# Two of the four loads of x issued by ScalarE in place of SyncE, in a graph-attention layer

## The reference

```python
x (8192, 64) f32;  adj (8192, 8192) int32, about 4 edges in a row;  W (64, 64);  a (128, 1)
h  = maximum(layernorm(x, axis=-1, eps=1e-5), 0)
Wh = h @ W
a1, a2 = a[:64, 0], a[64:, 0]
e  = leaky_relu((Wh @ a1)[:, None] + (Wh @ a2)[None, :], 0.2)
scores = where(adj > 0, e, -9e15)
attention = softmax(scores, axis=1)
out = x + elu(attention @ Wh)
```

## Time and profile before

| | us |
|---|---|
| median of three executions | 654.71 |
| the profiled execution, its own time | 654.69 |
| its span, first to last instruction | 652.8 |
| TensorE busy | 618.5 (95%) |
| VectorE busy | 614.8 (94%) |
| ScalarE busy | 623.9 (96%) |
| GpSimd busy | 81.6 (13%) |
| time in packets of the loads of `adj`, share of 16 DMA engines over the span | 98.6% |

### The profile page before, as it was taken

How to read it: one execution, slowest core, us unless ns; L and a number is a source line. 1 busy time by engine, 2 the same in 40 slices (tenths; PEclk the granted TensorE clock), 3 DMA queues, 4 the chain that set the end, 5 groups by cost and what they waited for, 6 DMA issues and landing times.

```text
span 652.8 us, 23363 instructions
## 1 busy us (share of the span) xinstructions
PE 618.5 (95%) x10422; PEld 607.1 (93%) x10422; DVE 614.8 (94%) x651; ACT 623.9 (96%) x357; POOL 81.6 (13%) x149
## 2 busy tenths in 40 slices
PE   4878999999999999999999999999999999989997
PEld 4748999999999999999899999999999999989997
DVE  5899999999999999889999999999999999999997
ACT  5799999899999999999999999999999999999992
POOL 7200200110110110100010110101010110011000
PEclk9987999999999999999999999999999999999999
DMA  9999999999999999999999999999999999999994
GB/s 173 109 108 109 110 108 108 110 109 109 109 108 108 107 107 108 108 108 108 107 108 108 108 108 107 108 107 108 108 108 107 108 107 108 108 108 107 107 97 132
DMA packets 27678, 71.81 MB, mean 110 GB/s; under 512 B 3200, under 2 KB 11136, under 8 KB 27648
## 3 DMA queue, kind: packets, MB, share of 16 engines
q0 software_dynamic: 18576, 67.12, 98.6%
q1 hardware_dynamic: 8608, 4.19, 2.4%
q10 hardware_dynamic: 464, 0.07, 0.1%
HBM read 270.60 MB, written 2.10 MB: 418 GB/s over the span
## 4 chain that ended last, share of the span: by engine, by line
ACT 53%; DMA 17%; PE 12%; issue 9%; DVE 7%; ACTq 1%; POOL 1%; DVEq 0%
ACT work L520 37%; DMA store<-in_adj 16%; ACT work L528 14%; DVE store L721 4%; PE psum L1083 3%; PE psum L1081 3%; PE psum L1061 2%; PE psum L1050 1%; PE psum L1028 1%; ACT last_steps L533 1%; DVE store L739 1%; DVE work L745 1%; DMA x_sb<-in_x 1%; PE psum L1018 1%; ACT V L512 1%
## 5 line engine op out<-in xcount | busy, mean ns | idle before, releaser
L520 ACT ACTIVATE work<-trow,Wh 128x4096 int8<-128x4096 f32 x128 | 494.6, 3867 | 0.0
L1081 PE MATMUL psum<-V,work 128*128 128x130 f16 x4096 | 479.3, 220 | 1.2 <-DVE work L745 1.2
L1083 PE MATMUL psum<-V,work 128*128 128x130 f16 x4096 | 479.2, 220 | 0.0
L1081 PEld LDWEIGHTS psum<-V,work 128*128 128x128 fp8e4 x4096 | 401.9, 98 | 1.5 <-issue 1.5
L1083 PEld LDWEIGHTS psum<-V,work 128*128 128x128 fp8e4 x4096 | 401.8, 98 | 0.0
L721 DVE TENSOR_SCALAR store<-store 128x4096 uint8<-128x4096 int8 x127 | 290.2, 2286 | 4.4 <-DMA store<-in_adj 4.4
L739 DVE SCALAR_TENSOR_TENSOR store<-work,store 128x1024 int32<-128x1024 int32 x128 | 156.5, 1222 | 12.7 <-ACT work L520 10.0
L528 ACT COPY work<-psum 128x1024 int32<-128x1024 int32 x128 | 147.5, 1155 | 7.6 <-PE psum L1061 7.4
L1061 PE MATMUL psum<-identb,store 128*128 128x128 bf16 x2048 | 135.7, 220 | 16.3 <-DVE store L739 13.4
L1061 PEld LDWEIGHTS psum<-identb,store 128*128 128x128 bf16 x2048 | 119.6, 98 | 20.1 <-DVE store L739 10.7
L443 POOL DMA_DIRECT2D store<-in_adj x127 | 71.2, 561 | 510.9 <-DVE store L721 503.3
(11 more groups left out here) (90 smaller groups left out, 146.6 us busy)
## 6 DMA issues: line engine op xcount, KB each, us to landing
store<-in_adj POOLq DMA_DIRECT2D x127, 512.0 KB, 27.6
x_sb<-in_x SPq DMA_DIRECT2D x4, 512.0 KB, 6.2
out_y<-x_sb SPq DMA_DIRECT2D x1, 1792.0 KB, 8.0
store<-in_adj POOLq DMA_DIRECT2D x2, 256.0 KB, 35.3
out_y<-x_sb SPq DMA_DIRECT2D x1, 128.0 KB, 6.0
out_y<-x_sb SPq DMA_DIRECT2D x4, 32.0 KB, 1.6
store<-in_L_gnn_W ACTq DMA_DIRECT2D x4, 16.0 KB, 5.3
a_sb<-in_L_gnn_a ACTq DMA_DIRECT2D x1, 0.5 KB, 4.2
```

The costliest lines, as they stand in the source:

```text
L520: nc.scalar.activation(sign[:, k % 2].bitcast(I8), trow[:, h * UW:(h + 1) * UW], ACT.Sign, bias=(Wh[:, B, 0:1] if isinstance(B, int) else ...
L1081: nc.tensor.matmul(sums_of[:, 0], up8[:, j // 2, j % 2], V[:, jb, 0:FP], start=begins and j == 0, stop=False, skip_group_check=True)
L1083: last = nc.tensor.matmul(sums_of[:, 1], down8[:, j // 2, j % 2], V[:, jb, VP:VP + FP], start=False, stop=stops and j == HB - 1, skip_grou ...
```

## The change

ScalarE issues the loads of the second and fourth quarter of `x`, ahead of its five small loads; SyncE issues those of the first and third. Tiles, semaphores, sizes and everything else stay. Lines behind the change move down by five in the changed kernel.

```diff
             def _(sp):
                 xs = x.rearrange("(g p b) f -> p g b f", p=P, b=2)
                 with nc.allow_non_contiguous_dma(reason="pairs of rows of x, 512 bytes each"):
-                    for r in range(NR):
+                    for r in range(0, NR, 2):
                         sp.dma_start(x_sb[:, out_of(r), :].rearrange("p (g b) f -> p g b f", b=2),
                                      xs[:, r * PR:(r + 1) * PR]).then_inc(s_x[r], 16)
...
             @block.scalar
             def _(act):
                 act.sem_inc(s_codeT, TWO)
+                xs = x.rearrange("(g p b) f -> p g b f", p=P, b=2)
+                with nc.allow_non_contiguous_dma(reason="pairs of rows of x, 512 bytes each"):
+                    for r in range(1, NR, 2):
+                        act.dma_start(x_sb[:, out_of(r), :].rearrange("p (g b) f -> p g b f", b=2),
+                                      xs[:, r * PR:(r + 1) * PR]).then_inc(s_x[r], 16)
                 with nc.allow_non_contiguous_dma(reason="128 numbers"):
                     act.dma_start(a_sb[:, :], a.rearrange("(c f) o -> f (c o)", c=2)).then_inc(s_a, 16)
```

## The result

The changed kernel takes 657.54 us (median of 5, 656.95 to 657.81) against 654.71 (654.53 to 655.17): ratio 1.0042, 95% interval 1.0031 to 1.0053. The profiled execution has a span of 655.7 us, 2.9 more than before, and ScalarE is the place to look first.

What follows compares the result with a forecast made beforehand. The prediction took the stream of `adj` loads, set by tile 0's landing, as the bound. First `adj` load +0.91 us, less 0.1 saved at start-up, gave +0.8: 654.7 + 0.8 = 655.5 us, range 654.4 to 657.2.

Steps and rivals of the forecast that it cites:

- What bounds the kernel: `adj` load stream: the end is tile 0's landing plus a fixed time, so delaying tile 0 delays the end one for one.
- The third rival: Start of the `adj` stream: bound by the tail of `x`, so up to 0.9 us later costs nothing; 654.7 us, chance 0.10.
- the cost of ScalarE's queue: ScalarE before the first minus means: two quarter issues take 1.24 us, 0.33 hidden in idle time, +0.91 us on the chain.
- the 0.1 us saved at the tail of `x`: Start-up of `adj` tile 0: its first packets no longer run into the tail of `x`; 0.1 us saved, bounds 0 and 0.4.
- The rival with long issues: ScalarE's issues of quarters: as long as SyncE's third and fourth, 2.74 us in place of 1.24; 657.1 us, chance 0.18.
- Order kept: SyncE's and ScalarE's transfers: served first come, first served, so quarter 0 costs 0; with short issues 655.5 us, chance 0.50.
- the 1.65 of the rival: Loads of quarters 0 and 1: both queues share the engines, row sums later by +1.65 us; 656.3 us, chance 0.22.
- the descriptor block locked for one issuer: ScalarE's first issues beside SyncE's large ones: by the skill page they could be long, the sum then the second rival's.
- The small loads' lateness: `a` and W behind quarter 3, landing near 10.6 to 11.0 us: ScalarE stands 0.3 to 0.5 us, covered by slack, cost nothing.

Runs made afterwards that it cites:

- the changed kernel with the load at quarter 0: Changed kernel with GpSimd issuing the first `adj` load as soon as quarter 0 of `x` has landed, ahead of the minus means; 654.59 us, ratio 0.9998.

## Why the prediction was wrong

The forecast was 655.5 us with a range up to 657.2, and 657.54 was measured. What bounds the kernel: right. The stream of `adj` starts late by what GpSimd's first centring is late, one for one (+2.0 in the changed kernel, +1.0 and +2.6 in two experiments), and the compute engines' slack covers the rest, as the changed kernel with the load at quarter 0 shows. The third rival, that the tail of `x` binds, holds on the early side alone: the first packets of `adj` started at 9.7 us beside that tail, so the earlier issues gained only 0.7 to 0.9 us, and the later ones cost their full delay.

**The step that failed** is the cost of ScalarE's queue, "with two quarters on each queue neither has a third". The two issues of quarters were sized right: 1.19 us against 1.24. But the queue does have a third issue, `a`, and I did not apply to it the wait that I had read off SyncE's third and fourth, because it is small. It cost 1.25 us more than before. The sum should have been 1.19 + 1.25 - 0.42 = +2.0 us. The 0.42 is the idle time in front of the first minus means (the activation behind the table load lets the next start after 0.11 us, so ScalarE was ready at 5.65); I had taken 0.33. With the 0.1 us saved at the tail of `x` that gives 656.6 us, so this step is 1.1 of the 2.0 us between forecast and result; the other 0.9 were in no term of the sum ("Not forecast" below), and they carried the result past the end of the range. The rival with long issues had the price, +2.4, but put it on the loads of `x`.

**Order kept** was wrong as well. In the trace of before, small loads of one queue stood behind quarters of the other, and I took that for first come, first served. Two quarters issued 0.09 us apart are served packet by packet. The page "DMA: Bandwidth & Descriptors" of the Trainium skill, section "Queues, rings and completion order", says that each DMA engine takes turns between its queues at packet granularity; 238 against 235 packets agree; the small loads that stood still in the earlier trace rows do not. The delay is 1.03 us and not the 1.65 of the rival, since quarter 0 was 473 packets ahead before the sharing was even and so let 619 packets of the other queue pass and not 1040. Alone it would have given 655.6 (the split with the small loads on SyncE); in the changed kernel it lies under ScalarE's.

The page "Perfetto Trace Analysis" of the Trainium skill, section "DMA Instruction — HWDGE (DVE, Sync)", has the descriptor block locked for one issuer. No row here shows a wait for that: SyncE's first issue ran from 0.75 to 1.20 us and ScalarE's from 0.84 to 1.30, each as long as the other.

The small loads' lateness, costed at nothing: right. The saving of 0.1 us at the tail of `x`: the first tile of `adj` took 7.6 us from issue to landing, 7.7 before.

**Not forecast**: what stands beyond the delay of the first `adj` load, 0.8 us in the changed kernel (0.9 with the 0.1 saved) and 0.7 in its second measurement. It has two parts. The last step of VectorE came up to 0.8 us later than the stream explains, in some profiles with the split and in some without (0.6 in the kernel before with small loads on SyncE); why is open. The last store of 32 KB landed in 1.5 us or in 1.9 to 2.3. It was late in exactly the six profiles in which ScalarE issues a quarter of `x` or two and the five small loads as well, and on time in the other seven, the split with the small loads on SyncE among them. In each of the six, 9 packets of the store started 0.15 to 0.34 us behind the others, at the moment at which an 8 KB packet of the instruction queue q14 ended (1.43 us after the issue in the changed kernel): they stood behind it. In the other seven no packet of the store came so late, and the q14 packet began 1.1 to 1.9 us after the issue. A longer program of ScalarE that moves the fetches of instructions would fit that; no run tests it.

## What to carry to other kernels

Splitting loads over two queues moved no byte sooner here, where the DMA engines were already busy; it made the first quarter later, since the second took half the packets for a while. Count every issue that an engine has to make before its first real work, and look how many large transfers stand ahead in the same queue: here the third issue waited, though it was half a kilobyte. And where a stream of loads bounds the kernel, look what stands ahead of its first load in the issuer's program: moving that one load ahead of the centring or to the landing of quarter 0 gained 0.7 to 0.9 us in the kernel before, and at the landing of quarter 0 it took back the changed kernel's whole loss (657.32 to 654.59 us), with the prologue as late as it was.

## What the runs showed of the hardware that was not expected

- An issue with two 512 KB loads ahead of it in its own queue ended only when 27 to 48% of the first had moved (285 to 500 of 1040 packets over the profiles); with at most one ahead, or with small loads ahead, it took 0.45 to 0.8 us. The other queue's load did not count: ScalarE's issues kept to 0.6 us while SyncE's fourth took 1.6.
- Two queues that both hold a quarter share packet by packet (238 and 235 in 0.7 us), yet the small loads of ScalarE's queue in the kernel before stood still through whole quarters of SyncE's. What decides between the two is open; in the first case the two issues ended 0.1 us apart, in the second the small ones ended 0.4 us and more behind a quarter's.
- The first packets of a stream issued by GpSimd took 1.17 us each in the kernel before, where its later ones and those of an early issue took 0.62.
